# Mixed layer on one core: the routed experts' up product with 256 moving columns, and the work around it moved between engines

## The reference, cut to what matters

```python
x = x + wkv(w, u, layernorm(x), ctx)            # 16 x 128 x 512
xf = layernorm(x).reshape(-1, 512)              # 2048 tokens
gates = softmax(xf @ gate_w + gate_b)           # 16 experts, the best 2 are kept
h = gelu(einsum('nd,edh->neh', xf, ew1) + eb1)  # 512 -> 128 per expert
eo = einsum('neh,ehd->ned', h, ew2) + eb2       # 128 -> 512
routed = einsum('ned,ne->nd', eo, combine)
hs = gelu(einsum('nd,sdh->snh', xf, sw1) + sb1) # two shared experts, 512 -> 2048
x = x + einsum('snh,shd->nd', hs, sw2) + sum(sb2) + routed
```

## Time and profile before

| | |
|---|---|
| median of 3 runs | 1015.77 us (1015.6 to 1016.11) |
| profiled execution | 1018.14 us, span 1016.3 us |
| PE busy | 874.2 us (86%) |
| DVE busy | 701.1 us (69%) |
| ACT busy | 537.1 us (53%) |
| POOL busy | 146.6 us (14%) |

### The profile page before, as it was taken

The page is one execution under the profiler, slowest core; times in us unless marked ns, Lnnn a source line. Parts: engine busy times, 40 slices in busy tenths (PEclk is TensorE's granted clock), DMA queues, the critical chain, the costliest instruction groups (busy, mean ns, idle before and its releaser), DMA issues.

```text
span 1016.3 us, 16771 instructions
## 1 busy us (share of the span) xinstructions
PE 874.2 (86%) x4182; PEld 720.5 (71%) x4183; DVE 701.1 (69%) x1382; ACT 537.1 (53%) x901; POOL 146.6 (14%) x174
## 2 busy tenths in 40 slices
PE   0008999999999999999999999999998999988496
PEld 0007778778777877887778778788886888876285
DVE  6996787884786969666787885565646677763382
ACT  2424776733538584443776733455544777762141
POOL 1001000021200000121000011111112344417400
PEclk9999999999999999999999999999997999999599
DMA  8212323249622323683323236555835566659634
GB/s 169 52 52 72 95 78 109 84 99 172 124 64 83 103 83 94 159 155 88 86 75 111 75 101 116 134 159 141 161 78 177 174 198 192 200 166 311 179 103 121
DMA packets 124507, 126.81 MB, mean 125 GB/s; under 512 B 13718, under 2 KB 87510, under 8 KB 124460
## 3 DMA queue, kind: packets, MB, share of 16 engines
q1 hardware_dynamic: 115676, 100.88, 39.1%
q0 software_dynamic: 8784, 25.37, 8.8%
HBM read 105.07 MB, written 21.14 MB: 124 GB/s over the span
## 4 chain that ended last, share of the span: by engine, by line
PE 78%; issue 6%; DVE 6%; SPq 2%; DMA 2%; DVEq 2%; ACT 1%; ACTq 1%; another core or an unknown queue 0%; POOL 0%; POOLq 0%
PE up L500 13%; PE up L501 13%; PE up L502 13%; PE acc L540 11%; PE acc L544 11%; PE acc L541 11%; DVEq L290 2%; DMA w_raw<-in_L_ffn_sw 1%; PE acc L500 1%; PE up L649 1%; SPq L393 1%; PE acc L502 1%; PE acc L501 1%; SPq L409 1%; DMA xg<-xn_rows,idx 1%
## 5 line engine op out<-in xcount | busy, mean ns | idle before, releaser
L540 PE MATMUL acc<-w2hi,hhi 128*128 128x512 f32 x512 | 202.4, 395 | 25.3 <-issue 25.3
L500 PE MATMUL up<-xs,w1hi 128*128 128x512 f32 x512 | 205.0, 400 | 11.4 <-ACT xs L774 6.0
L541 PE MATMUL acc<-w2lo,hhi 128*128 128x512 f32 x512 | 201.1, 393 | 4.5 <-issue 4.5
L501 PE MATMUL up<-xs,w1hi 128*128 128x512 f32 x512 | 201.6, 394 | 1.2 <-issue 1.2
L502 PE MATMUL up<-xs,w1lo 128*128 128x512 f32 x512 | 201.6, 394 | 0.7 <-issue 0.7
L906 DVE TENSOR_TENSOR hlo<-hf,hhi 128x512 fp32r<-128x512 f32 x128 | 88.1, 688 | 126.0 <-ACT hhi L730 66.5
L544 PE MATMUL acc<-w2hi,hlo 128*128 128x512 f32 x512 | 138.1, 392 | 2.9 <-issue 2.9
L730 ACT ACTIVATE hhi<-up,b_col 128x512 fp32r<-128x512 f32 x128 | 88.4, 691 | 97.8 <-PE up L502 51.7
L540 PEld LDWEIGHTS acc<-w2hi,hhi 128*128 128x128 f32 x512 | 96.8, 189 | 53.3 <-issue 33.6
L500 PEld LDWEIGHTS up<-xs,w1hi 128*128 128x128 f32 x512 | 97.5, 190 | 31.6 <-ACT xs L774 7.0
L544 PEld LDWEIGHTS acc<-w2hi,hlo 128*128 128x128 f32 x512 | 97.0, 189 | 24.7 <-issue 4.4
(11 more groups left out here) (214 smaller groups left out, 1295.6 us busy)
## 6 DMA issues: line engine op xcount, KB each, us to landing
w_raw<-in_L_ffn_sw SPq DMA_DIRECT2D x256, 256.0 KB
expert_rows<-ysb SPq DMA_DIRECT2D x48, 256.0 KB, 2.3
X<-in_x SPq DMA_DIRECT2D x16, 256.0 KB, 7.0
vin<-in_ctx SPq DMA_DIRECT2D x16, 256.0 KB
xn_rows<-kn POOLq DMA_DIRECT2D x16, 256.0 KB, 8.3
e2raw<-in_L_ffn_ew SPq DMA_DIRECT2D x16, 256.0 KB
ew_sb<-in_L_ffn_ew SPq DMA_DIRECT2D x16, 256.0 KB, 6.8
out<-X SPq DMA_DIRECT2D x16, 256.0 KB, 3.9
```

The costliest lines, as they stand in the source:

```text
L500: nc.tensor.matmul(o, lhs[0], rhs[0], start=start, stop=False)
L501: nc.tensor.matmul(o, lhs[0], rhs[1], start=False, stop=False)
L540: nc.tensor.matmul(acc[t][:], hh, w2hi[:, slot], start=first, stop=False)
L541: nc.tensor.matmul(acc[t][:], hh, w2lo[:, slot], start=False, stop=False)
```

## The change

- The tokens' two parts go side by side into one tile `xgp`, and each of the four groups of the up product becomes one matmul of `e1hi` with 256 columns (both parts) and one of `e1lo` with 128. The bank then holds two halves that have to be added.
- VectorE adds them with a `tensor_reduce` into a new tile `rs` in SBUF, and both Gelus read `rs`.
- GpSimd rounds the expert's weights (`e1hi`), with its own `value_load`; its program is written out for all 48 slots and gathers with columns of `xrow`, so the copies to `idx` go.
- ScalarE copies every slot's result to `ysb`, from four banks `acc0` to `acc3`. VectorE copies none.

```diff
-                for k in range(KC):
-                    last = splits(r_bank[i][:, 0:P], (e1hi[:, i, k], e1lo[:, i, k]), (xghi[:, i, k], xglo[:, i, k]),
-                                  k == 0, k == KC - 1)
+                need(pe, rsum, s - 1)
+                for k in range(KC):
+                    nc.tensor.matmul(r_bank[i][:, 0:2 * P], e1hi[:, i, k], xgp[:, i, k], start=k == 0, stop=False)
+                    last = nc.tensor.matmul(r_bank[i][:, 0:P], e1lo[:, i, k], xgp[:, i, k, 0], start=False,
+                                            stop=k == KC - 1)
...
-                need(pe, rye[i], y_taken(s, static) - 1)
-                splits(y_bank[i][:], (rhi[:, i], rlo[:, i]), (e2hi[:, e], e2lo[:, e]), True, True).then_inc(ry, 1)
+                need(pe, rye, s - 3)
+                splits(acc[static % 4][:], (rhi[:, i], rlo[:, i]), (e2hi[:, e], e2lo[:, e]), True, True).then_inc(ry, 1)
...
-            def routed_w1(s, static):
-                e = act.value_load(rvT[0:1, bass.ds(s, 1)], min_val=0, max_val=E - 1)
-                need(act, rup, s - 1)
-                nc.scalar.copy(e1hi[:, static % 2], ew1_sb[:, e]).then_inc(r1hi, 1)
...
-                act.wait_ge(rup, s + 1)
+                act.wait_ge(rsum, s + 1)
                 need(act, ry, s - 1)
-                nc.scalar.activation(rhi[:, i], r_bank[i][:, 0:P], ACT.Gelu, bias=b).then_inc(rhh, 1)
+                nc.scalar.activation(rhi[:, i], rs[:, i], ACT.Gelu, bias=b).then_inc(rhh, 1)
...
-                nc.scalar.copy(ysb[:, n], y_bank[1][:]).then_inc(rye[1], 1)
+                nc.scalar.copy(ysb[:, n], acc[n][:]).then_inc(rye, 1)
...
-                n = static % 4
-                V.tensor_copy(idx[:, n:n + 1], xrow[:, bass.ds(s + 4, 1)]).then_inc(idx_ok, 1)
 
             def routed_h(s, static):
                 i = static % 2
+                dve.wait_ge(rup, s + 1)
+                need(dve, rff, s - 1)
+                V.tensor_reduce(rs[:, i], r_bank[i][:, 0:2 * P].rearrange("p (a n) -> p n a", a=2), AX.X, ALU.add)\
+                    .then_inc(rsum, 1)
                 dve.wait_ge(rhh, s + 1)
                 dve.wait_ge(rff, s + 1)
...
-                V.tensor_copy(ysb[:, n], y_bank[0][:]).then_inc(rye[0], 1)
...
+            def routed_w1(s):
+                e = pool.value_load(rvT[0:1, s:s + 1], min_val=0, max_val=E - 1)
+                need(pool, rup, s - 1)
+                G.tensor_copy(e1hi[:, s % 2], ew1_sb[:, e]).then_inc(r1hi, 1)
...
+            for s in range(2, SLOT_TILES):
+                routed_w1(s)
+                if s + 4 < SLOT_TILES:
+                    gather(s + 4)
```

More of the change, by code:

```diff
@@ L109, in mixed_layer @@
         sb("hf_rest", [P, 3 * RING * D - EH * D], where=routed_mem)
-        xghi = sb("xghi", [P, 2, KC, P], f32r, routed_mem)
-        xglo = sb("xglo", [P, 2, KC, P], f32r, routed_mem)
+        xgp = sb("xgp", [P, 2, KC, 2, P], f32r, routed_mem)
         e1hi = sb("e1hi", [P, 2, KC, P], f32r, routed_mem)
@@ L117, in mixed_layer @@
         ysb = sb("ysb", [P, 4, D], where=routed_mem)
+        rs = sb("rs", [P, 2, P], where=routed_mem)
         routed_mem.close()
@@ L214, in mixed_layer @@
         bslot = sb("bslot", [P, NS])
-        idx = sb("idx", [P, 4], i32)
         slot_mem = ExitStack()
@@ L350, in uses, with routed_rounds @@
             return (c - static) // 3 + static // 3 + 1 if not isinstance(c, int) else c // 3 + 1
-        def routed_rounds(eng, w1, x, h, y, parity, start=lambda: None):
+        def routed_rounds(eng, w1, x, h, y, start=lambda: None):
             def one(s, static):
@@ L360, in one @@
                     x(s + 2, static + 2)
-                if (not isinstance(s, int) or s) and (static - 1) % 2 == parity:
+                if not isinstance(s, int) or s:
                     y(s - 1, static - 1)
@@ L861, in routed_x @@
                 need(act, rup, s - 1)
-                nc.scalar.copy(xghi[:, i], t_bank[i][:].rearrange("p (k n) -> p k n", k=KC)).then_inc(rxh, 1)
+                nc.scalar.copy(xgp[:, i, :, 0], t_bank[i][:].rearrange("p (k n) -> p k n", k=KC)).then_inc(rxh, 1)
             def routed_h(s, static):
@@ L867, in routed_h @@
                 act.wait_ge(tvec.sem, tvec.at(0))
-                act.wait_ge(rup, s + 1)
+                act.wait_ge(rsum, s + 1)
                 need(act, ry, s - 1)
-                nc.scalar.activation(rhi[:, i], r_bank[i][:, 0:P], ACT.Gelu, bias=b).then_inc(rhh, 1)
+                nc.scalar.activation(rhi[:, i], rs[:, i], ACT.Gelu, bias=b).then_inc(rhh, 1)
                 act.wait_ge(tvec.sem, tvec.at(0))
                 need(act, rhl, s - 1)
-                nc.scalar.activation(rf[:, i], r_bank[i][:, 0:P], ACT.Gelu, bias=b).then_inc(rff, 1)
+                nc.scalar.activation(rf[:, i], rs[:, i], ACT.Gelu, bias=b).then_inc(rff, 1)
             def routed_y(s, static):
@@ L1358, in final @@
                         V.tensor_copy(bslot[:], misc[:, 2 * P:2 * P + NS]).then_inc(tvec.sem, 1)
-                        after(tvec, 0, "xrow")
-                        V.tensor_copy(idx[:], xrow[:, 0:4]).then_inc(idx_ok, 1)
                 schedule(q, step, head, half, mid, tile, late, final)
@@ L1385, in routed_x @@
                 need(dve, rup, s - 1)
-                V.tensor_tensor(xglo[:, i], t_bank[i][:].rearrange("p (k n) -> p k n", k=KC), f(xghi[:, i]),
+                V.tensor_tensor(xgp[:, i, :, 1], t_bank[i][:].rearrange("p (k n) -> p k n", k=KC), f(xgp[:, i, :, 0]),
                                 ALU.subtract).then_inc(rxl, 1)
-                n = static % 4
-                V.tensor_copy(idx[:, n:n + 1], xrow[:, bass.ds(s + 4, 1)]).then_inc(idx_ok, 1)
             def routed_h(s, static):
                 i = static % 2
+                dve.wait_ge(rup, s + 1)
+                need(dve, rff, s - 1)
+                V.tensor_reduce(rs[:, i], r_bank[i][:, 0:2 * P].rearrange("p (a n) -> p n a", a=2), AX.X, ALU.add)\
+                    .then_inc(rsum, 1)
                 dve.wait_ge(rhh, s + 1)
@@ L1533, in _, with gather @@
             pool.wait_ge(tvec.sem, tvec.at(0))
-            def gather(s, static):
-                n = static % 4
+            def gather(s):
+                n = s % 4
                 need(pool, rT, s - 3)
-                pool.wait_ge(idx_ok, 1 if isinstance(s, int) and s < 4 else s - 2)
                 apart(pool)
                 pool.indirect_dma_start(out=xg[:, n], out_offset=None, in_=xn_dram[:, :],
-                                        in_offset=bass.IndirectOffsetOnAxis(ap=idx[:, n:n + 1], axis=0))\
+                                        in_offset=bass.IndirectOffsetOnAxis(ap=xrow[:, s:s + 1], axis=0))\
                     .then_inc(g_in[n], 16)
[L1544 to L1549, removed]
+            def routed_w1(s):
+                e = pool.value_load(rvT[0:1, s:s + 1], min_val=0, max_val=E - 1)
+                need(pool, rup, s - 1)
+                G.tensor_copy(e1hi[:, s % 2], ew1_sb[:, e]).then_inc(r1hi, 1)
+            for s in range(4):
+                gather(s)
+            pool.wait_ge(ew_in, 16 * E)
+            pool.wait_ge(down_done, HOLD)
+            pool.wait_ge(h_lo, HOLD)
+            routed_w1(0)
+            routed_w1(1)
+            gather(4)
+            gather(5)
+            for s in range(2, SLOT_TILES):
+                routed_w1(s)
+                if s + 4 < SLOT_TILES:
+                    gather(s + 4)
             for n in range(4):
```

24 lines of the change are left out of this document (6 added, 18 removed).

## The result

The changed kernel takes 1054.53 us (median of four runs, 1051.59 to 1060.64), the kernel before 1015.68 beside it: ratio 1.0397, interval 1.0344 to 1.0451. That is +39 us, where +47 was forecast. The profiled execution took 1052.82 us, its span is 1051.2, 34.9 more than before.

A forecast was written before the change was run, and what follows sets the result against it. TensorE was taken to bound the routed stage, with VectorE's closed round bounding it after the change: 41 + 1.7 + 4 = +47 us on 1018.1 gives 1065; the median stands 2.4 lower, so 1063 us, range 1036 to 1090.

The forecast's parts named there:

- TensorE bounds the stage before: Routed stage before the change: TensorE busy 10.23 of a 10.70 us loop pass, 2.48 us a slot, plus one gap.
- The paired product: TensorE's up product: 4 matmuls of 256 and 4 of 128 columns take 1.0 us a slot instead of 1.37.
- The sum: VectorE's new addition of 256 PSUM values into 128: 0.42 us, between 0.34 and 0.7.
- The closed round: VectorE's slot from sum through ScalarE's Gelus, rlo, e1lo, xgp to next sum: 3.64 us against 2.67; ten passes +41 us.
- the shorter 0.84: Rival: register load costs 0.84 in the loop as outside; round 3.26, +26 us, 1042 us; chance 0.09.
- The loop's branch: First slot of each pass shows 1.71 instead of 1.22 us; half of that 0.49 added, making a pass 14.8.
- The clock: TensorE's gaps may lower its clock; 0.18 us over the round for half of 44 slots: +4 us.
- under 70%: Sign of being right: TensorE under 70% busy in the stage, waiting at the first up matmul for xgp.
- GpSimd: Its e1hi copy takes 0.63 us, its slot 2.7 to 3.1, under 3.64; gathers issued four slots ahead: adds nothing.
- GpSimd's rival, the port: GpSimd's copy shares the SBUF port with e1lo, holding it back 0.63 us: +28, 1091 us; chance 0.05.
- The stages outside unchanged: Sign of being right: the stages outside the routed stage keep their length.

The follow-up runs named there:

- the early load in the kernel before: Kernel before, with VectorE's register load of the expert's number for slot s+2 put ahead of rlo's wait: 988.7 us, ratio to kernel before 0.9918.
- the moves alone: Changed kernel without the paired product and the sum, three products of 128 columns, Gelus from PSUM; copies stay where the change put them: 995.01 us, ratio 0.9975.
- other order: Changed kernel with VectorE's slot in the order sum, e1lo, rlo, xgp, so e1lo runs during ScalarE's Gelus: 993.58 us, ratio to kernel before 0.9955.
- early load: Changed kernel, VectorE reading the expert's number of slot s+2 ahead of slot s's sum instead of behind rlo: 1006.05 us, ratio to kernel before 1.0102.
- the changed kernel again: The changed kernel unaltered, the last experiment, on a chip other than the result's: 1037.47 us, ratio to kernel before 1.042.
- other order, gather later: Changed kernel, VectorE in order sum, e1lo, rlo, xgp, and GpSimd gathering slot s+3 instead of s+4 behind its copy: 979.47 us, ratio 0.9832.

## Why the prediction was right

The bound, the mechanism and the sign were right, and 1063 was 8.5 us over. Point by point:

- *TensorE bounds the stage before.* Right as to the slots: with the early load in the kernel before a slot takes 2.48 us, the sum of TensorE's three parts. The gap of each pass was VectorE's open load; moving it gave 0.8% on the kernel before.
- *The paired product.* Costed at 1.0 us, measured 0.94, with errors that cancel: the matmul of 256 columns takes 0.19 and 0.17 to the next start, over the 0.16 set as its upper bound, and the one of 128 behind it 0.06 instead of 0.114.
- *The sum.* 0.42, measured 0.41, though it jumps 128 values in PSUM; its groups row has 407, 415 and 417 ns as least, median and longest of 48.
- *The closed round.* 3.64 forecast, 3.59 measured, with errors that cancel. The step from the sum to ScalarE is 0.18, not 0.08. `rhi` to `rlo` is 0.79, not 0.71: both Gelus are longer from SBUF (0.40 against 0.37 in the earlier trace rows). And `rlo` to `e1lo` is 1.00, not 1.22. I had taken 1.22 from ten passes before and called the shorter 0.84 a rival; it is 0.84 outside the loop (794.09 to 794.93) and 1.00 inside, between the two. The other 0.22 lay in the load itself. VectorE's instruction handling in the kernel before, in the first slot of a pass and in the third:

```profile
L1377 DVEq TENSOR_LOAD <-rvT x1: 1005/1005/1005, 852.2 to 852.2; - x1
L1377 DVEq TENSOR_LOAD <-rvT x1: 518/518/518, 857.7 to 857.7; - x1
```

  In the third slots of the ten passes TENSOR_LOAD takes 496 to 521 ns, inside the changed kernel's loop 307 to 323. The step that was mis-sized is thus the price of one load, carried over from a kernel in which it took 0.21 us longer. Why it does so there, and in "the moves alone", stays open.
- *The loop's branch.* The extra half of 0.49 a pass did not come. The pass is 14.35, which is 4 x 3.59; forecast was 14.8. The 0.49 of the earlier trace rows was the longer TENSOR_LOAD as well (1005 against 518 ns). From the first `rlo` inside the loop to the first behind it ten passes grew by 38.1 us, where 41 was forecast.
- *The clock.* The +4 did not come: granted clock 1.00 in the loop with TensorE busy for 14.04 of 20 us. This, the load and the branch's extra are the mis-sized terms: +46.7 forecast for the stage, +39.2 measured (38.1 in the loop, 1.1 outside it). TensorE's busy share, 70 to 71%, missed the sign of "under 70%" by a hair.
- *GpSimd.* Its copy takes 0.63, as worked out from rows 9, and cost nothing in this kernel. But "a gather is issued four slots ahead, nothing" overlooked that the copy then stands behind the gather's own wait. In the changed kernel that had no effect, since each copy was over 3.5 to 3.8 us before its `e1lo`; in the run "other order" the copy became the bound.
- *GpSimd's rival, the port.* The loop shows none of it, since copy and `e1lo` don't overlap there. In slot 2 they do, on VectorE and on GpSimd:

```profile
791.16 1.13 DVE L1363 TENSOR_TENSOR e1lo<-ew_sb,e1hi 128x512 fp32r<-128x512 f32 x1 [0.57 <-issue]
```

```profile
791.11 0.62 POOL L1523 CAST e1hi<-ew_sb 128x512 fp32r x1
```

`e1lo` started 0.05 behind the copy and took 1.13 instead of 0.69. The same came four times more, each time with the copy begun first (early load: 1.11, 1.01 and 1.02 at 910.27, 913.56 and 916.74; the changed kernel again: 1.12 at 799.40). Where `e1lo` had begun first, eight times in the run "early load", it kept its 0.69. That bears out the Trainium skill's rule ("SBUF — State Buffer", "Who interferes with whom"); `xgp`, which reads PSUM, ran beside a copy in the run "other order, gather later" (850.54, copy at 850.93) in its usual 0.69. For the copy, the Trainium skill's "GPSIMD Engine Reference", section 3.1, has 769 ns for 512 elements; the trace has 630.
- *The stages outside unchanged.* Not quite: −4.8 us, one chunk more ahead of the hole in the last chunks. The gain belongs to executions with the hole; in the last experiment, which has none, the ratio is 1.042. The runs of one kernel differ by up to 9 us (1051.59 to 1060.64), more than one such chunk; whether the hole makes that too was not tried.

## What to carry to other kernels

Before a step is put between two engines, write down the closed round it makes: from the engine's first instruction through the other engine and back, with everything that the program order queues behind the wait. An engine's register load is paid in full when it stands behind an instruction that waits and no long instruction lies between the two; so put work that needs no wait between a result handed over and the wait for the answer, and look where in the round the load comes to lie, since moving it can cost as well as gain. Where an engine has taken on a second job, check what its copy is queued behind, and don't trust a named releaser when its event lies well ahead of the start: count off which copy belongs to which instruction. A copy that really released its reader ended 0.14 to 0.15 us before it here, in four runs.

## What the runs showed that I had not expected

- From chip to chip the end of the program changes, not the routed stage: same stage (165.5 and 165.5), 17 us apart in time. The hole was there in both profiles on the result's chip (106.9 and 102.1 us from the last `rlo` to the end) and in none of the ten on the three other chips (80.4 to 82.4 us). Whether the chip makes it isn't shown. The DMA engines are busy for 0.98 ahead of the hole and 0.67 in it, and for 0.94 throughout where there is none:

```profile
955.00:980.00 25.00, 22.74 (x93) 17.92 (x93) 12.89 (x20) 9.18 (x16) 19.21 (x20) 0.96 0.98 324
980.00:1000.00 20.00, 9.14 (x18) 4.73 (x18) 2.49 (x5) 2.38 (x5) 12.36 (x13) 0.53 0.67 197
```

```profile
960.00:985.00 25.00, 24.18 (x100) 19.90 (x101) 16.61 (x27) 12.40 (x22) 17.38 (x17) 0.93 0.94 314
985.00:1000.00 15.00, 15.00 (x68) 12.43 (x67) 12.32 (x20) 6.45 (x12) 11.64 (x12) 1.00 0.94 296
```

The first fence is the changed kernel's first profile, the second the same kernel on the other chip. What makes the hole was not tried.
- One register load costs VectorE 0.84 to 1.0 us from the start of the instruction ahead of it, though TENSOR_LOAD itself takes 0.31; the rest is register steps around it. In other kernels of this case the same TENSOR_LOAD takes up to 1.04 us, and the cost grows by as much.
- A small Gelu (128 columns) is 0.03 us longer from SBUF than from PSUM, and the chain of two grew by 0.08.
